# Turning the quantised hidden rows with VectorE and DMA in a fused attention and FP4 feed-forward kernel

## The reference

```
Q = xpos(X @ W_Q);  K = xpos(X @ W_K, downscale);  V = X @ W_V
p = softmax(Q K^T) * 0.9 ** |n - m|;   x = layernorm(X + p V)
xq = quant(x)                      # blocks of 16, scale = max/6, values on the E2M1 grid
h  = silu(xq @ quant(w_gate).T) * (xq @ quant(w_up).T)      # 704 wide
x  = layernorm(x + quant(h) @ quant(w_down).T)
```

## Time and profile before

| | |
|---|---|
| median of 3 runs | 987.44 us (986.03 to 988.91) |
| the profiled execution | 987.3 us |
| its span, first to last instruction | 985.5 us |
| PE / DVE / ACT / POOL busy | 97% / 88% / 66% / 84% |
| granted TensorE clock | 0.998 of full speed |
| DMA moved | 111.27 MB; the main queue 34.8% of 16 engines |

### The profile page before, as it was taken

One profiled execution on the slowest core, in us unless ns is written; L12 is line 12 of the kernel. 1 busy time (PEld: TensorE's weight loads), 2 busy tenths in 40 slices (PEclk: granted clock), 3 DMA queues, 4 the chain that ended last, 5 costly groups with the idle time before them and its releaser, 6 DMA issues.

```text
span 985.5 us, 20524 instructions
## 1 busy us (share of the span) xinstructions
PE 960.3 (97%) x6002; PEld 868.2 (88%) x6002; DVE 862.8 (88%) x1995; ACT 649.6 (66%) x1576; POOL 830.5 (84%) x1034
## 2 busy tenths in 40 slices
PE   8999999999999999999999999999999999999996
PEld 7788898989998899998989889898898989889986
DVE  6979888988988988888998888898898888889986
ACT  3655766676666677666676666667666666767754
POOL 5988888898888889889888888889888888887754
PEclk9999999999999999999999999999999999999999
DMA  9124235243442425314352423523334342323300
GB/s 317 44 86 128 88 97 172 91 129 93 130 144 80 137 85 176 109 55 151 104 180 82 130 91 102 172 91 113 107 102 147 106 134 81 99 98 105 115 18 28
DMA packets 116112, 111.27 MB, mean 113 GB/s; under 512 B 12576, under 2 KB 93728, under 8 KB 114080
## 3 DMA queue, kind: packets, MB, share of 16 engines
q1 hardware_dynamic: 115312, 108.91, 34.8%
q10 hardware_dynamic: 688, 1.05, 0.3%
HBM read 69.53 MB, written 40.37 MB: 112 GB/s over the span
## 4 chain that ended last, share of the span: by engine, by line
PE 68%; DVE 12%; POOL 6%; issue 4%; DMA 4%; ACT 3%; SPq 2%; DVEq 0%; POOLq 0%; ACTq 0%
PE ps_g L641 10%; PE ps_g L642 9%; PE ps_g L643 9%; PE ps_oy L641 7%; PE ps_oy L643 7%; PE ps_oy L642 7%; PE ps_s L641 4%; PE ps_s L642 4%; PE ps_s L643 4%; PE ps_t L650 3%; DMA landing<-parking 3%; POOL q_l L2508 2%; POOL h L2485 2%; PE ps_oy L650 1%; DVE turned L1876 1%
## 5 line engine op out<-in xcount | busy, mean ns | idle before, releaser
L2485 POOL TENSOR_TENSOR h<-h,hsc 128x704 f32<-128x704 f32 x126 | 168.6, 1338 | 50.4 <-DVE h L1850 36.6
L2600 POOL TENSOR_TENSOR prob<-prob,decay_t 128x512 f32<-128x512 f32 x128 | 164.8, 1297 | 1.9 <-ACT prob L1289 1.9
L641 PE MATMUL ps_oy<-v_h,pt_h 128*128 128x256 f32 x512 | 149.3, 292 | 0.5 <-DVE pt_l L1886 0.4
L641 PE MATMUL ps_g<-wgu_h,xqt_h 128*128 128x480 f32 (+1 forms) x380 | 148.7, 391 | 0.6 <-DVE h L1819 0.5
L642 PE MATMUL ps_oy<-v_l,pt_h 128*128 128x256 f32 x512 | 144.7, 283 | 0.0
L643 PE MATMUL ps_oy<-v_h,pt_l 128*128 128x256 f32 x512 | 144.6, 282 | 0.0
L643 PE MATMUL ps_g<-wgu_h,xqt_l 128*128 128x480 f32 (+1 forms) x380 | 142.4, 375 | 0.0
L642 PE MATMUL ps_g<-wgu_l,xqt_h 128*128 128x480 f32 (+1 forms) x380 | 142.1, 374 | 0.0
L641 PE MATMUL ps_s<-k_h,q_h 128*128 128x512 f32 x256 | 102.8, 402 | 0.0
L1801 DVE SCALAR_TENSOR_TENSOR th<-th,ps_g 128x240 f32<-128x240 f32 x183 | 71.6, 394 | 33.9 <-ACT th L1219 31.4
L642 PE MATMUL ps_s<-k_l,q_h 128*128 128x512 f32 x256 | 100.2, 391 | 0.0
(11 more groups left out here) (276 smaller groups left out, 3103.6 us busy)
## 6 DMA issues: line engine op xcount, KB each, us to landing
parking<-turned SPq DMA_DIRECT2D x122, 256.0 KB, 2.0
landing<-parking SPq DMA_DIRECT2D x488, 64.0 KB, 2.0
rope_t<-rope SPq DMA_DIRECT2D x15, 1024.0 KB, 5.8
xres<-x SPq DMA_DIRECT2D x64, 128.0 KB, 2.1
out<-yout SPq DMA_DIRECT2D x63, 128.0 KB, 2.0
xin<-x_t SPq DMA_DIRECT2D x14, 512.0 KB, 4.5
first_rope<-rope SPq DMA_DIRECT2D x2, 512.0 KB, 8.2
decay_t<-decay SPq DMA_DIRECT2D x1, 960.0 KB, 12.2
```

The lines of the kernel that those rows point to most:

```text
L641: pe.matmul(dst, a_h, b_h, start=(start and i == 0), stop=False)
L2485: return tt(blocks(dst), blocks(src), sc[:, which, at:at + n].unsqueeze(2).to_broadcast([P, n, QB]), ALU.mult)
L2600: tt(prob[:, keys], prob[:, keys], decay_t[:, lo:lo + CW], ALU.mult).then_inc(decayed, 1)
```

## The change

Six things are changed. (1) For tiles 0 to 58 `h_transposes`, `h_high` and `h_low` are replaced: VectorE transposes the 32x32 squares of the quantised h (`turn_h`, 640 columns and then 128, into the tile `turned`, which the probabilities use too), SyncE parks them in DRAM and lands them in four transfers (`park_h`, `land_h`, tile `h_landing`), ScalarE makes the high part in one cast of 768 columns (`h_landed_high`), and VectorE the low part in two subtractions, both with two SBUF operands (`h_landed_low`). These last two and `down` now stand one step later than before relative to the grid step, at the end of it. Tiles 59 to 63 keep the old way. (2) `down` of tiles 0 to 58 writes the second bank of `ps_t`. (3) ScalarE computes Silu for every tile, straight into h, and VectorE multiplies by up in one instruction for each part (`gate_times_up`); `gated` is gone. (4) `landed_copied` is gone: `landed_low` on VectorE reads `landing` itself, and so has two SBUF operands. (5) The second norm's mean, squares, variance, inverse and shift are made one step later (tile `six`). (6) The orders of all five queues are new, and some semaphores are merged or new.

```diff
-SMOOTH = LAST_TILE - 2
+LAST_TURNED = LAST_TILE - 5
+def turns(i):
+    return 0 <= i <= LAST_TURNED
-        th = sb("th", [P, F])
+        h_landing = sb("h_landing", [P, QUADS * FC * QUAD])
+        h_parking = nc.dram_tensor("h_parking", [2, P, QUADS * FC * QUAD], F32, kind="Internal").ap()
+        def y_at(i):
+            return ps_t[:].rearrange("p a b n -> p a (b n)")[:, 1, D:2 * D] if turns(i) else ps_y[:, 0:D]
+            def park_h(i):
+                if turns(i):
+                    sp.wait_ge(ht_done, 2 * i + 2)
+                    wait(sp, h_landed, 16 * QUADS * (i - 1))
+                    sp.dma_start(h_parking[i % 2], h_turned).then_inc(h_parked, 16)
+            def land_h(i):
+                if turns(i):
+                    sp.wait_ge(h_parked, 16 * (i + 1))
+                    wait(sp, htl_done, 2 * i)
...
+                    for c in (0, 2, 1, 3):
+                        sp.dma_start(h_landing[c * QUAD:(c + 1) * QUAD, :].rearrange("p (a x) -> p a x", a=QUADS),
+                                     rows[c]).then_inc(h_landed, 16)
...
 # ScalarE
-            def tanh(i, r):
+            def silu(i, r):
...
-                    nc.scalar.activation(th[:, part(r)], gate_up_at(i, r)[:, 0], ACT.Tanh if i < SMOOTH else ACT.Silu,
-                                         scale=0.5 if i < SMOOTH else 1.0).then_inc(tanh_done, 1)
+                    nc.scalar.activation(h[:, i % 2, part(r)], gate_up_at(i, r)[:, 0], ACT.Silu).then_inc(silu_done, 1)
-            def landed_copied(i):
...
+            def h_landed_high(i):
+                if turns(i):
+                    act.wait_ge(h_landed, 16 * QUADS * (i + 1))
+                    wait(act, y_done, i)
+                    nc.scalar.copy(keys_by_quad(ht_h), h_landed_at).then_inc(hth_done, 2)
...
 # VectorE
+            def gate_times_up(i, r):
+                if live(i):
+                    wait(dve, silu_done, PARTS * i + r + 1)
+                    hv = h[:, i % 2, part(r)]
+                    tt(hv, hv, gate_up_at(i, r)[:, 1], ALU.mult).then_inc(h_done, 1)
+            def turn_h(i, g):
+                if turns(i):
+                    dve.wait_ge(hq_done, 2 * i + g + 1)
+                    if g == 0:
+                        for half in range(2):
+                            wait(dve, parked[half], 16 * (crossing(i + 3) if crosses(i + 3) else 0))
+                        nc.vector.transpose(h_turned_to[:, 0:FC - 1], h[:, i % 2, 0:(FC - 1) * P]).then_inc(ht_done, 1)
+                    else:
+                        nc.vector.transpose(h_turned_to[:, FC - 1:FC], h_last[:]).then_inc(ht_done, 1)
+            def h_landed_low(i):
+                if turns(i):
+                    dve.wait_ge(hth_done, 2 * i + 2)
+                    high = keys_by_quad(ht_h)
+                    tt(keys_by_quad(ht_l), h_landed_at[:, :, 0:FC - 1, :], high[:, :, 0:FC - 1, :].bitcast(F32), ALU.subtract)
+                    rest = high[LAST:P, :, FC - 1, :]
+                    tt(rest, h_landed_at[LAST:P, :, FC - 1, :], rest.bitcast(F32), ALU.subtract).then_inc(htl_done, 2)
...
             def turn(i, g):
+                    if turns(i - 4):
+                        dve.wait_ge(h_parked, 16 * (i - 3))
...
             def landed_low(i):
-                    dve.wait_ge(copied, crossing(i))
-                    tt(pt_l[:, keys, :], ps_t[:, 1], pt_h[:, keys, :].bitcast(F32), ALU.subtract)\
-                        .then_inc(ptl_done[1], 1)
+                    tt(keys_by_quad(pt_l[:, keys, :]), landed_half(1), keys_by_quad(pt_h[:, keys, :]).bitcast(F32),
+                       ALU.subtract).then_inc(ptl_done[1], 1)
 # orders, one of eight: the VectorE step with j = 6, from the x grid on
                     x_grid(three)
                     rot_mul(*rot, 0)
                     rot_mul(*rot, 1)
+                    xqt_low(three)
                     h_shift(four)
-                    xqt_low(three)
-                    h_grid(four)
                     first_residual(two)
+                    h_grid(four)
+                    h_landed_low(five)
                     row_max(now)
-                    gated(three, 0)
-                    silu(three, 0)
-                    h_low(four, 0)
-                    gated(three, 1)
-                    gated(three, 2)
-                    silu(three, 1)
-                    silu(three, 2)
-                    h_low(four, 1)
+                    gate_times_up(three, 0)
+                    turn_h(four, 0)
+                    turn_h(four, 1)
+                    second_residual(five)
+                    gate_times_up(three, 1)
+                    gate_times_up(three, 2)
                     x_max(two)
```

More of the change, by code:

```diff
@@ L551, in step @@
                 if j == 0:
[L552 to L568, removed]
+                    park_h(five)
+                    land_h(five)
                     park(one, 0)
@@ L955, in step @@
                     scores(now, 0)
-                    down(five)
+                    scores(now, 1)
                     values_product_first(two)
@@ L2111, in step @@
                     x_reciprocals(three)
-                    h_scales(four)
-                    turn(one, 1)
-                    second_residual(five)
+                    landed_low(two)
                     h_reciprocals(four)
-                    landed_low(two)
+                    row_max(now)
                     x_shift(three)
@@ L2120, in step @@
                     rot_mul(*rot, 1)
+                    xqt_low(three)
+                    h_shift(four)
+                    first_residual(two)
+                    h_grid(four)
+                    h_landed_low(five)
+                    turn_h(four, 0)
+                    turn_h(four, 1)
+                    gate_times_up(three, 0)
+                    gate_times_up(three, 1)
+                    x_max(two)
+                    second_residual(five)
+                    gate_times_up(three, 2)
+                elif j == 3:
+                    x_scales(three)
+                    x_reciprocals(three)
+                    turn(one, 1)
+                    h_max(four)
+                    landed_low(two)
+                    h_scales(four)
+                    turn(one, 0)
+                    x_shift(three)
+                    row_inverse(two)
+                    h_reciprocals(four)
+                    x_grid(three)
+                    row_max(now)
+                    v_low(c_v, 0)
+                    v_low(c_v, 1)
                     h_shift(four)
@@ L2259, in step @@
                     x_grid(three)
+                    rot_mul(*rot, 0)
+                    rot_mul(*rot, 1)
+                    xqt_low(three)
+                    h_shift(four)
+                    first_residual(two)
+                    h_grid(four)
+                    h_landed_low(five)
+                    row_max(now)
+                    gate_times_up(three, 0)
+                    turn_h(four, 0)
+                    turn_h(four, 1)
+                    second_residual(five)
+                    gate_times_up(three, 1)
```

1264 lines of the change are left out of this document (598 added, 666 removed).

## The result

The changed kernel takes 1089.1 us (median of 4 runs, 1087.12 to 1091.0) against 988.16 us (986.03 to 988.91) for the kernel before on the same chip: ratio 1.1025, 95% interval 1.0997 to 1.1054. That is 101 us slower, and 88 us above the upper end of the predicted range. The profiled execution took 1088.26 us, its span is 1086.5 us.

A forecast was written before the change was run, and what follows sets the result against it. The prediction took TensorE, 97% busy, to bound the kernel. It expected no gain in 19 light steps and 0.57 us in each of 40 heavy ones: 985.5 - 23 = 962.5, so 964 us as median, range 946 to 1001 (forecast's own 952 to 982).

The forecast's parts named there:

- Heavy steps: The 40 steps with projection: GpSimd's 14.84 us is the largest sum, 0.57 below 15.41, saving 23 us.
- the whole scores and values work: The moved down product on TensorE: this work lies ahead and covers late operands, so the move costs nothing.
- TensorE, 0.65 us a tile: Six transposes of h leave TensorE's stream in each of 59 steps: at most 38.4 us comes off.
- rival A: All steps: everything hides, VectorE meets GpSimd's gaps and TensorE stays the bound, 949 us; chance 0.17.
- The shared access: VectorE's two-SBUF-operand low parts and GpSimd delay each other: 0.96 us a step on VectorE, 0.41 on GpSimd.
- Rival B: Small subtraction of `h_landed_low` waits for a whole 1.28 us GpSimd instruction: 1018 us, or 1000 in three of four steps; chance 0.28.
- ScalarE, nothing on the path: Two Exp/Silu table loads a step, 2.57 us, hide in ScalarE's idle 4.7 us; bounds nothing and 2.57 a step.
- Rival C: ScalarE's table loads, between PSUM results and their users, lie on the path: about 987 us; chance 0.10.
- DMA and SyncE, nothing: h's added DRAM transfers and SyncE's issues cost nothing; bound 1 us a step if the probabilities land late.
- The turn's wait on the shared tile: `turn` waits until parked h has left `turned`; over 2.5 us of VectorE instructions cover a 2 us transfer.
- Moving parts between steps, nothing: Moving the down product and the second norm to other places costs nothing, since the instructions are the same.

The follow-up runs named there:

- a_hpsum: Changed kernel with both subtractions of `h_landed_low` reading PSUM in place of the landed tile: 1035.93 us, ratio 1.0482 to the kernel before.
- a_nosq: Changed kernel with Tanh for Silu, low parts from PSUM, no DRAM way for h, and VectorE's squares cut to 32 and 32 columns: 997.06 us.
- b_few: Kernel before with two of the six transposes of h in each tile left on TensorE: 982.74 us, ratio 0.993.
- a_rest: Changed kernel with only the small 64x128 subtraction of `h_landed_low` reading PSUM: 1053.28 us, ratio 1.0648 to the kernel before.
- b_silu: Kernel before with Silu and one VectorE multiplication in every tile, old orders: 1105.22 us, ratio 1.1166.
- a_both: Changed kernel with Tanh for Silu in tiles 0 to 60 and the low parts read from PSUM: 1014.1 us, ratio 1.027.

## Why the prediction was wrong

The sum of the runs, in the order in which they were peeled off (in another order the shares would be somewhat different): 1089.1; small subtraction -36; h's large one -17; `landed_low` -18; table loads -4; DRAM way -16; squares 0 to 1; that is 997, still 8 to 9 above the kernel before.

**The step that failed** is in "Heavy steps": "The largest, 14.84, is 0.57 below 15.41". I added up each engine's work, put the shared access into VectorE's sum, and took the fullest engine for the step. A tile takes 16.47 us, while VectorE's work in it is (101.35 + 104.00)/236 x 16.47 = 14.33 and GpSimd's (97.95 + 98.13)/236 x 16.47 = 13.68. My own sums, averaged over six heavy and two light steps, were (6 x 14.36 + 2 x 12.57)/8 = 13.91 and, with 0.41 on each of GpSimd's 13.85 and 9.90, 13.27. So the works were sized to within about 0.4 us and none fills the step. In a heavy step, 14.84 by my sum and 17.4 by the estimate above, the chain leaves TensorE almost altogether; from 334.94 to 359.91 us TensorE has 0.45 us of it:

```profile
340.77 0.82 DVE ht_l L1885
...
341.61 1.26 DVE ht_h L1887
...
342.90 1.24 DVE nmax L1945
...
356.34 1.05 DVE ht_h L1887
...
360.46 0.21 PE ps_t L692
```

Here the contended subtraction stands ahead of the row maximum, and so ahead of the exponential, in VectorE's list. What sets a step is thus a path through several engines, in which each instruction waits for the one before; in a light step it closes to a ring. The chain of the changed kernel there (start us, us, what):

```profile
990.90 1.76 DVE ht_l L1885
...
992.68 0.30 DVE ht_h L1887
...
993.02 0.39 PE ps_t L691
...
993.52 0.12 PE ps_t L693
...
1000.94 0.43 PE ps_oy L700 x2
...
1001.40 0.38 ACT xqt_h L1306
...
1002.14 0.48 DVE ps_oy L1954
1002.63 0.80 DVE h L1849
...
1003.45 0.89 DVE h L1855
...
1004.60 1.78 DVE ht_l L1885
```

From one `h_landed_low` to the next it is 13.70 us: low part of h, down, scores, values, turned x, x's high part, the h grid, and the low part again. The 0.96 us that the low part takes over its 0.82 is in the ring. It does not follow that each delay counts in full: with the 0.96 gone (`a_hpsum`) the step fell by 0.3 only, to the second path through the table loads. And `down` now needs a result made just ahead of it, though I had written that its cover was "the whole scores and values work". That work is no cover here: VectorE's list has the low part of h behind the low part of x, which itself waits for scores, values and the turned x.

- *TensorE, 0.65 us a tile.* The transposes are gone from the chain, and most of their time from TensorE's work: in `a_nosq` a light step is 12.88 with a gap of 0.92, so the work in it is 11.96, 0.5 below 12.47. But it does not reach the end: `b_few` shows that even in the old orders only about a quarter of such a relief arrives. TensorE had 68% of the chain before, not all of it. So rival A, which needs the whole relief, was out in those orders already.
- *The shared access.* My 0.96 us a step on VectorE was too low by a quarter: over the durations without contention (0.289, 0.815, 0.67 us) the three groups have 48.7, 15.7 and 12.7 us, 77 in all or 1.3 a tile. My two equal terms were wrong in kind: each large subtraction has 0.2 to 0.3 on average, and the small one 0.83. On GpSimd I had 0.41 a tile, 24 us. Its h instruction alone rose from 1338 to 1502 ns, 21 us, but short ones were held up too (0.19 us becomes 0.77 at 355.61), and its busy time rose from 830.5 to 881.7 us with the same 1034 instructions: 51 us, twice my term.
- *Rival B* had the place, the mechanism and the event ("the small one waits for a whole 1.28 us instruction"), in 41 of 59 tiles, or seven in ten; its sign holds. Its price, 13 to 31 us slower than before, was too low, because it too was reckoned by the fullest engine; by `a_rest` the small subtraction alone is 36, and the kernel is 101 slower. What I set against it, that VectorE must wait for GpSimd's `h_quantised` anyway, was wrong: VectorE's list puts `h_landed_low` right there, but it has other work too, and what waits is TensorE: 28.9 us on PE and 48.0 on its weight loads for L1887.
- *ScalarE, nothing on the path:* right for this kernel within the noise, 2 to 4 us, but by luck as much as by reasoning. "ACT's 16% of air" was my ground, and `b_silu` has about as much and pays 121 us. Rival C does not set this kernel's time; in `a_hpsum`'s light steps, with a slower part out of the way, both loads are on the path.
- *DMA and SyncE, nothing:* wrong by 16 us in `a_both`, inside the bound of 1 us a step. The queue's share is 44.7% where I had about 49. The turn's wait on the shared tile was 2.1 us in total, as costed. Later landings are the likely price.
- *Moving parts between steps, nothing:* wrong, as far as is known: with h's and the second half's low parts from PSUM, no loads and no DRAM way, the new orders, with what moved in them, are 8 to 9 us slower than the old with less work.

## What to carry to other kernels

When a pipeline's engines are all near 85 to 97%, do not take the fullest engine's sum for the step: follow the ring from one late result to the same in the next step, add every new delay to it, and look how far behind the next ring is, for that is all that can be won back on the first. A short VectorE instruction with two SBUF operands is a dear place to meet GpSimd, since it pays for the rest of a GpSimd instruction whatever its own size; keep one operand in PSUM, or keep such instructions out of the stretch in which GpSimd works. And move an operation in one engine's list only with its partners in the others.

## What the runs showed of the hardware

- A VectorE subtraction of 64 x 128 with two SBUF operands took 0.289 us alone and 1.27, or up to 2.50, beside one GpSimd instruction; with one operand in PSUM it took 0.295 on average, and no longer beside GpSimd's h instruction (`a_rest`, 0.29 at 300.61, GpSimd from 299.94 to 301.73). GpSimd's instruction was held up as well, 1.28 to 1.89 us.
- Alternating Exp and Silu costs 1283 ns for each switch, in all 121 of them, and no longer gap shows: the load of 990.56 ends at 991.84, and the exponential starts at 991.86. The Trainium skill (ScalarE: Activation LUTs, What ACT_TABLE_LOAD costs) has the same 1283 ns and a drain of about 1380 ns besides; no row here shows that drain.
- The Trainium skill (GPSIMD Engine Reference, Key points) names the contention for two SBUF inputs; these runs agree and give it a price, up to one whole instruction of the other engine each time, and 71 us of this kernel.
